# Gated attention's triangles on row tiles of the array, V on column tiles, and the softmax sums taken by ScalarE

## The chip, the core and the metric

One core of a Trainium2 chip runs the whole program, one launch for all 32 batch rows. The metric is the device time of that core in microseconds, from its first to its last instruction, with a little around it. Lower is better.

## What is computed

A decoder layer on x of shape 32 x 256 x 256 (row, token, feature), all in float32, with three residual blocks:

```
x = x + gated_attention(layernorm(x))      # 4 heads, 64 slots; q and k of 32, v of 64 per head
x = x + cross_attention(layernorm(x), ctx) # 16 heads of 16, ctx has 77 tokens a row, a mask of keys
x = x + moe(layernorm(x))                  # 8 experts of rank 64, the best 2 of 8 weighted
```

The gated attention runs two linear recurrences over the tokens, with slot weights exp(s - cumulative logsumexp(s)). The kernel writes each as a product with a causal triangle inside blocks of 128 tokens plus a state that is carried from the first block to the second. The first triangle is A = K Q^T per head (over 32 features), the second is P = E qn^T per head (over 64 slots, E = exp(s), qn the normalised softmax of the first result). In the cross attention, a softmax over 77 context tokens is taken for each of 16 heads, and its product with V is divided by the softmax's sum.

## The kernel before

**Stages.** A batch row goes through four stages, one per iteration: N (norm, projections, convolution of the gated attention), A (its attention and output), X (cross attention), F (mixture of experts). In iteration i the five instruction queues hold the N steps of row i, the A steps of row i-1, the X steps of row i-2 and the F steps of row i-3; there are 35 iterations. Each engine has its own function `body` with an order of these steps written out by hand, and runs them strictly in this order. Steps on different engines are tied by one semaphore per step. `upto(r, n)` is the count that a step with n increments a row has reached after row r. `g_mm`, `g_out`, `g_lo`, `g_store` project the context to K and V for all rows at once, during the first iterations.

**PSUM.** All eight banks of 128 x 512 float32 have fixed users: `E0` (all products of stage N, turns of E and v), `A0` and `A1` (stage A), `X0` (`x_turn`, `x_q`, the scores `x_s`, `x_proj`), `X1` (turned probabilities and turned output), `X2` (the product with V), `F0` and `F1` (stage F). So within X, everything that goes through `X0` follows one upon another: `x_turn` of a row can't start before `x_out` (VectorE) has read the `x_proj` of the row before.

**Products.** Projections split each operand in a high and a low half of type float32r and add three products (`mm_halves`). The others are float32 products, and each such product stands as two matmuls and two weight loads in the trace. `a_A` is one product of 128 x 512 per block c: the 32 features of each of 4 heads lie on the 128 partitions, and `q_bd` holds the four heads' q on a block diagonal of zeros, so that heads don't mix. `a_P` does the same with 64 slots and `qn_bd`, 256 columns at a time. VectorE multiplies both with a triangle (`a_maskA`, `a_maskP`).

**Cross attention.** A row has 8 units u = (c, q): a block c of 128 tokens and 4 heads. `x_s` makes the scores of a unit in `X0` (three matmuls of 308 columns), `x_soft` (VectorE) takes the maximum, `x_prob` (ScalarE) makes four exponentials of 128 x 77 into `prob`, where a head has 80 columns, and only then can `x_s` of the next unit overwrite `X0`. `x_pt` turns `prob` in 10 tiles of 128 columns a block, and `x_av` multiplies each turned tile, as the stationary operand, with the 34 or 51 columns of `Vbd` that its heads have: 16 features a head and a column of ones that gives the softmax's sum. `x_rs` and `x_o` (VectorE) divide, `x_ot` turns the output (TensorE) and copies it (ScalarE), `x_otl` makes the low half, `x_proj` projects.

**DMA.** One queue (SyncE) loads x and the mask, stores the output, and fills `Vbd` (12 small transfers a row) and the K tiles from a copy of K and V in HBM.

## Time and profile before

| | |
|---|---|
| median of 3 runs | 1520.54 us (1518.21 to 1521.38) |
| profiled execution | 1518.72 us |
| its span, first to last instruction | 1516.6 us |
| TensorE matmul busy | 96% |
| VectorE, ScalarE, GpSimdE busy | 80%, 63%, 55% |
| granted TensorE clock, mean | 0.989 of 2.4 GHz |

The profile is of one execution. A busy share says how much of the span had an instruction of the engine under way. Matmuls are pipelined and their ends are modelled, so a duration of a matmul is longer than its distance to the next; what a matmul costs is read from the distance of the starts. PE is TensorE, PEld its weight loads, DVE VectorE, ACT ScalarE, POOL GpSimdE, SP the DMA queue's engine.

### The profile page before, as it was taken

The numbers are of one execution on the slowest core, as the hardware profiler recorded it, in microseconds if no ns is written. First come the engines' busy times: TensorE is split into PE (matmuls) and PEld (weight loads), VectorE is DVE, ScalarE is ACT, GpSimd is POOL, SyncE is SP. The second block draws the span as 40 slices with busy tenths as digits, with TensorE's granted clock in tenths as the row PEclk, the third lists the DMA queues.
The fourth block names the chain that finished last, engine by engine and source line by source line (L and its number), as shares of the span: only waits on it lengthen the run. The fifth ranks groups of instructions, "written<-read, shape, count | busy, mean of one in ns | idle before, by whom it ended". The sixth has DMA issues, their size and how long they took to land.

```text
span 1516.6 us, 31405 instructions
## 1 busy us (share of the span) xinstructions
PE 1456.9 (96%) x10520; PEld 1291.4 (85%) x10520; DVE 1217.1 (80%) x3006; ACT 961.4 (63%) x2531; POOL 828.6 (55%) x937
## 2 busy tenths in 40 slices
PE   5798999999999999999999999999999999999975
PEld 3577989889889988988989888889988989989764
DVE  3668888888888888888888888888888888888642
ACT  3456666766666667666666766666667666666541
POOL 2355555656665565565556656655565565556420
PEclk9999999999999999999999999999999999999987
DMA  8230100011110001111100011110001111000000
GB/s 250 98 100 18 24 10 23 17 24 24 25 24 15 18 16 24 24 24 24 24 10 23 17 24 24 24 24 10 23 16 24 24 24 24 21 13 18 17 7 14
DMA packets 113102, 45.03 MB, mean 30 GB/s; under 512 B 86192, under 2 KB 109104, under 8 KB 112944
## 3 DMA queue, kind: packets, MB, share of 16 engines
q1 hardware_dynamic: 112944, 43.03, 11.3%
q8 instruction: 86, 1.41, 0.4%
q14 instruction: 72, 0.59, 0.1%
HBM read 26.74 MB, written 16.25 MB: 28 GB/s over the span
## 4 chain that ended last, share of the span: by engine, by line
PE 91%; DVE 3%; issue 2%; POOL 1%; ACT 1%; DMA 1%; SPq 0%; POOLq 0%; DVEq 0%; ACTq 0%
PE bank L444 76%; PE bank L450 7%; PE bank L685 5%; PE bank L770 2%; PE bank L532 1%; DVE a_conv L887 1%; PE bank L738 0%; DVE a_rC L909 0%; ACT x_prob L1331 0%; SPq L433 0%; DMA x_prob<-in_ctxT 0%; DVE x_nmax L1013 0%; DMA x<-in_x 0%; PE bank L541 0%; DVE x L1035 0%
## 5 line engine op out<-in xcount | busy, mean ns | idle before, releaser
L1331 ACT ACTIVATE x_prob<-bank,x_nmax 128x77 f32<-128x77 f32 x1024 | 248.5, 329 | 51.2 <-DVE x_nmax L1013 50.2
L1013 DVE TENSOR_REDUCE x_nmax<-bank 128x4 f32<-128x308 f32 x256 | 120.1, 469 | 109.8 <-PE bank L444 106.0
L1344 ACT ACTIVATE x_probT<-bank 128x256 f32<-128x256 f32 (+1 forms) x256 | 112.2, 438 | 98.3 <-PE bank L685 98.1
L1497 POOL TENSOR_TENSOR a_orinv<-a_ove,mhalf 128x8 f32<-128x8 f32 x32 | 65.1, 2035 | 199.1 <-DVE a_ove L952 199.1
L444 PE MATMUL bank<-x_Vbd,x_probT 128*128 128x34 f32 (+1 forms) x1280 | 162.5, 267 | 0.7 <-DVE x_o L1027 0.7
L887 DVE SCALAR_TENSOR_TENSOR a_conv<-a_raw,cw,a_conv 128x256 f32<-128x256 f32 x384 | 155.0, 478 | 7.5 <-POOL a_conv L1459 7.5
L444 PEld LDWEIGHTS bank<-x_Vbd,x_probT 128*128 128x128 f32 x1280 | 158.0, 192 | 1.1 <-DVE x_o L1027 1.1
L685 PE MATMUL bank<-ident,x_prob 128*128 128x128 f32 x640 | 114.6, 277 | 0.4 <-ACT x_prob L1331 0.3
L909 DVE RECIPROCAL a_rC<-bank 128x512 f32<-128x512 f32 x32 | 107.1, 3348 | 0.6 <-PE bank L444 0.6
L912 DVE TENSOR_TENSOR a_AT<-bank,tri 128x512 f32<-128x512 f32 x128 | 87.7, 685 | 23.9 <-PE bank L444 23.9
L444 PE MATMUL bank<-x_K_bd,x_Q_stack 128*128 128x308 f32 x256 | 94.5, 369 | 8.6 <-ACT x_prob L1331 5.2
L685 PEld LDWEIGHTS bank<-ident,x_prob 128*128 128x128 f32 x640 | 79.5, 145 | 21.9 <-ACT x_prob L1331 9.7
L1450 POOL TENSOR_SCALAR a_E<-a_E 128x512 f32<-128x512 f32 x32 | 62.1, 1940 | 54.9 <-ACT a_E L1230 54.9
L1459 POOL TENSOR_SCALAR a_conv<-a_raw,cw 128x256 f32<-128x256 f32 x128 | 59.1, 479 | 56.3 <-ACT a_raw L1224 56.3
L1535 POOL TENSOR_TENSOR f_s<-f_s,f_wt 128x512 f32<-128x512 f32 x64 | 66.7, 1043 | 39.0 <-DVE f_wt L1098 25.0
L1349 ACT ACTIVATE x_oT_hi<-bank 128x512 fp32r<-128x512 f32 x32 | 19.2, 598 | 107.2 <-PE bank L450 107.2
L1510 POOL TENSOR_TENSOR x_K_bd<-x_K_stack,groupmask 128x308 fp32r<-128x308 f32 x128 | 86.0, 704 | 0.0
L1434 POOL TENSOR_TENSOR x_rstd<-x_ve,mhalf 128x2 f32<-128x2 f32 x32 | 22.9, 715 | 114.6 <-DVE x_neg L842 114.6
L444 PE MATMUL bank<-x_negmask,ident_bf 128*128 128x308 bf16 x256 | 79.6, 311 | 0.0
L444 PE MATMUL bank<-x_KT_lo_bd,x_Q_stack 128*128 128x308 f32 x256 | 77.4, 302 | 0.0
L1513 POOL TENSOR_TENSOR x_KT_lo_bd<-x_KT_lo,headmask 128x616 fp32r<-128x616 f32 x64 | 76.8, 1221 | 0.0
L444 PE MATMUL bank<-fwo_hi,f_sT_hi 128*128 128x256 f32 x256 | 75.2, 294 | 1.5 <-ACT f_sT_hi L1378 1.5
(271 smaller groups left out, 5264.0 us busy)
## 6 DMA issues: line engine op xcount, KB each, us to landing
x<-in_x SPq DMA_DIRECT2D x32, 256.0 KB, 2.6
out<-x SPq DMA_DIRECT2D x32, 256.0 KB, 2.2
x_K_stack<-k_hi SPq DMA_DIRECT2D x64, 77.0 KB, 2.6
k_hi<-f_sT_hi SPq DMA_DIRECT2D x5, 512.0 KB, 2.8
k_lo<-f_sT_lo SPq DMA_DIRECT2D x5, 512.0 KB, 3.8
v_tok<-x_probT SPq DMA_DIRECT2D x10, 256.0 KB, 3.4
x_KT_lo<-k_lo SPq DMA_DIRECT2D x32, 77.0 KB, 2.3
x_Vbd<-v_tok SPq DMA_DIRECT2D x128, 9.6 KB
```

The costliest lines, as they stand in the source:

```text
L444: return pe.matmul(out, lhsT, rhs, start=start, stop=stop, skip_group_check=True)
L450: ins = pe.transpose(dst[:, k * T + c * P:k * T + (c + 1) * P], src[:, c, k * P:(k + 1) * P], ident[:])
L685: ins = pe.transpose(X1[:, i * P:(i + 1) * P], prob[:, t * P:(t + 1) * P], ident[:])
L887: stt(conv[:, j, :], raw[:, j, i:i + T], cw[:, j, i:i + 1], conv[:, j, :], ALU.mult, ALU.add).then_inc(on.a_conv, 1)
L909: dve.reciprocal(flat(rC[r % 2]), E0[:, :]).then_inc(on.a_rC, 1)
L912: return tt(dst, src.rearrange("p (h t) -> p h t", h=H), tri.rearrange("p (o t) -> p o t", o=1).broadcast_to([P, H, P]), ALU.mult)
L1013: dve.tensor_reduce(nmax[:, u % 2, :], X0[:, 0:UH * S2].rearrange("p (h s) -> p h s", h=UH), AX.X, ALU.min).then_inc(on.x_max, 1)
L1331: ins = act.activation(prob[:, col:col + S2], X0[:, i * S2:(i + 1) * S2], ACT.Exp, scale=-1.0, bias=nmax[:, u % 2, i:i + 1])
L1344: act.activation(probT[:, g[0]:g[-1] + 1, :].rearrange("p h t -> p (h t)"), X1[:, 0:len(g) * P], ACT.Copy).then_inc(on.x_pT, 1)
L1510: pool.tensor_tensor(K_bd[:, q], K_stack[r % 2][:, q:q + 1, :].broadcast_to([P, UH, S2]), spread(groupmask[:], S2), ALU.mult)
L1513: ins = pool.tensor_tensor(KT_lo_bd[:, f], KT_lo[r % 2][:, f:f + 1, :].broadcast_to([P, HB, S2]), spread(headmask[:], S2), ALU.mult)
L1535: pool.tensor_tensor(fs[:, c, :].rearrange("p (e q) -> p e q", e=NE), fs[:, c, :].rearrange("p (e q) -> p e q", e=NE), spread(wt[:, c, :], ...
```

## The change

- `a_A` and `a_P` no longer use a block diagonal over all partitions. Each product takes 64 partitions (`rows`), the upper and the lower half in turn, and writes the upper's result to one bank and the lower's to the other: 4 products of 256 columns for `a_A`, 8 of 128 columns for `a_P`. `q_bd` shrinks to two heads a half, `qn_bd` and `qn_last` become one plain copy `qnT`. Both blocks of a row are now one step.
- `x_av` swaps its operands: `Vbd` (64 columns, four heads, zeros elsewhere) is stationary and `probT`, which now holds both blocks' tokens, moves with 256 columns. The output has 64 partitions (the column tile i) and is already turned. There are 12 products a row in 2 steps, in place of 20 in 8.
- The column of ones goes. `x_prob` gives each exponential an accumulator output, `xsum`. VectorE takes its reciprocal (`x_rs`), GpSimdE spreads it over the 16 features of a head (`x_rse`), TensorE turns that (`x_rt`, four turns in place of those of `x_ot`), ScalarE copies it, and VectorE multiplies the product with V by it (`x_on`); the high half is then copied from SBUF (`x_ot`).
- `a_conv`, `a_rc`, `f_yy` and `x_kbd` are cut in pieces that other steps can stand between.
- Every engine has a new order. On TensorE, `x_proj` moves from the end of an iteration to the beginning of the next, `a_ktok` the other way, and the turns `x_pt` start later. On SyncE, `Vbd` is filled last in an iteration, for a row of stage N.

```diff
-VW = 3 * (HD + 1)
+VS, VW = 6, 4 * HD
...
-        q_bd = [sb(f"a_q_bd_{i}", [P, H, T]) for i in range(2)]
+        q_bd = [sb(f"a_q_bd_{i}", [P, 2, T]) for i in range(2)]
...
-        AT = sb("a_AT", [P, TC, H, P])
+        AT = sb("a_AT", [P, 2, TC * 2, P])
...
-        qn_bd = sb("a_qn_bd", [P, 2, 2, T])
-        qn_last = sb("a_qn_last", [P, 2, P])
+        qnT = sb("a_qnT", [P, 2, T])
...
-        g_ctx = [sb(f"g_ctx_{i}", [P, GW]) for i in range(3)]
-        Vbd = [sb(f"x_Vbd_{i}", [P, NT, VW]) for i in range(2)]
+        Vbd = [sb(f"x_Vbd_{i}", [P, 2, VS, VW]) for i in range(2)]
...
-        probT = sb("x_probT", [P, NT, P])
+        probT = sb("x_probT", [P, NT, T])
+        xsum = sb("x_sum", [P, TC, NH])
         xrs = sb("x_rs", [P, TC, NH])
-        xo = sb("x_o", [P, TC, D])
+        rse = sb("x_rse", [P, TC, D])
+        rsT = sb("x_rsT", [P, KC, T])
+        xo = sb("x_o", [P, KC, T])
...
-            (Vbd[0][:], a["vones"]), (Vbd[1][:], a["vones"]),
...
-                N(g_store, 0); N(g_store, 1); N(x_load); N(g_store, 2); N(g_store, 3); L(a_load); A(x_vbd)
-                F(f_store); N(x_kin)
+                N(g_store, 0); N(x_load); N(g_store, 1); N(g_store, 2); N(g_store, 3); L(a_load); F(f_store)
+                N(x_kin); N(x_vbd)
...
-            def a_A(r, c):
...
+            def a_A(r):
+                pe.wait_ge(on.a_qbd, upto(r))
+                if r > 0:
+                    pe.wait_ge(on.a_oT, upto(r - 1))
+                    pe.wait_ge(on.a_oTl, upto(r - 1))
+                pe.wait_ge(on.a_ktok, upto(r))
+                for c in range(TC):
+                    for i in range(2):
+                        rows = slice(i * P // 2, (i + 1) * P // 2)
+                        ins = mm((A0 if i == 0 else A1)[:, c * D:(c + 1) * D], qkr[r % 2][rows, 1, c * P:(c + 1) * P],
+                                 q_bd[r % 2][rows, :, c * P:(c + 1) * P])
+                        if c == TC - 1:
+                            ins.then_inc(on.a_A_ps, 1)
...
-            def a_P(r, c):
...
+            def a_P(r):
+                pe.wait_ge(on.a_qnT, upto(r))
+                for c in range(TC):
+                    for f in range(2):
+                        for i in range(2):
+                            rows = slice(i * P // 2, (i + 1) * P // 2)
+                            ins = mm((A1 if i == 0 else A0)[:, c * D + f * P:c * D + (f + 1) * P],
+                                     ET[r % 2][rows, f, c * P:(c + 1) * P], qnT[rows, f, c * P:(c + 1) * P])
+                            if c == TC - 1 and f == 1:
+                                ins.then_inc(on.a_P_ps, 1)
...
-            def x_av(r, u):
-                c, q = divmod(u, QU)
-                if u == 0:
+            def x_av(r, g):
+                if g == 0:
                     if r > 0:
-                        pe.wait_ge(on.x_o, upto(r - 1, TC))
+                        pe.wait_ge(on.x_on, upto(r - 1))
                     else:
                         pe.wait_ge(on.g_v, 2 * NG)
                     pe.wait_ge(vbd_in[r % 2], loaded(r, len(V_PIECES)))
-                elif q == 0:
-                    pe.wait_ge(on.x_o, upto(r, TC, c))
-                pe.wait_ge(on.x_pT, upto(r, NU, u + 1))
-                for t in GROUPS[q]:
-                    h, w = first_head(t) * (HD + 1), tile_heads(t) * (HD + 1)
-                    ins = mm(X2[:, h:h + w], probT[:, t, :], Vbd[r % 2][:, t, 0:w], start=(t == 0),
-                             stop=(t == NT - 1))
+                pe.wait_ge(on.x_pT, upto(r, NU, QU + 2 * (g + 1)))
+                for j in range(VS // 2):
+                    for i in range(2):
+                        t = g * NT // 2 + 2 * i + j
+                        ins = mm(X2[i * VW:(i + 1) * VW, g * T:(g + 1) * T], Vbd[r % 2][:, g, i * VS // 2 + j, :],
+                                 probT[:, t, :], start=(j == 0), stop=(j == VS // 2 - 1))
                 ins.then_inc(on.x_av_ps, 1)
-            def x_ot(r):
-                pe.wait_ge(on.x_o, upto(r, TC))
-                turn(X1, xo).then_inc(on.x_oT_ps, 1)
+            def x_rt(r):
+                pe.wait_ge(on.x_rse, upto(r, TC))
+                pe.wait_ge(on.x_pT, upto(r, NU))
+                for f in range(KC):
+                    for c in range(TC):
+                        ins = pe.transpose(X1[:, f * T + c * P:f * T + (c + 1) * P],
+                                           rse[:, c, f * P:(f + 1) * P], ident[:])
+                ins.then_inc(on.x_rT_ps, 1)
...
-                A(a_vtok); N(g_mm, 0); N(g_mm, 1); A(a_ktok); A(a_A, 0); X(x_turn); A(a_A, 1); A(a_state)
-                N(g_mm, 2); N(a_turn); X(x_q); F(f_turn); A(a_ok); N(a_qk); X(x_s, 0); F(f_gate); F(f_u0)
-                N(g_mm, 3); X(x_pt, 0); X(x_s, 1); F(f_lg); N(a_v); A(a_qt); X(x_s, 2); F(f_v0); N(a_s)
-                X(x_s, 3); A(a_P, 0); A(a_P, 1); X(x_pt, 1); X(x_av, 0); X(x_s, 4); X(x_pt, 2); A(a_o)
-                X(x_av, 1); X(x_pt, 3); F(f_st, 0); X(x_s, 5); N(g_mm, 4); N(a_g); F(f_u1); X(x_pt, 4)
-                X(x_av, 2); X(x_s, 6); F(f_v1); X(x_pt, 5); X(x_av, 3); N(g_mm, 5); X(x_s, 7); N(g_mm, 6)
-                N(a_c); X(x_pt, 6); A(a_ot); N(g_mm, 7); X(x_av, 4); F(f_st, 1); X(x_pt, 7); X(x_av, 5)
-                X(x_av, 6); X(x_av, 7); N(a_et); A(a_wo); X(x_ot); F(f_yy); X(x_proj)
+                F(x_proj); A(a_vtok); A(a_A); N(g_mm, 0); X(x_turn); A(a_state); N(g_mm, 1); X(x_q); N(a_turn)
+                F(f_turn); A(a_ok); X(x_s, 0); F(f_gate); N(a_qk); F(f_u0); N(g_mm, 2); X(x_s, 1); F(f_lg)
+                N(a_v); N(g_mm, 3); A(a_qt); X(x_s, 2); F(f_v0); N(a_s); X(x_s, 3); X(x_pt, 0); A(a_P)
+                X(x_pt, 1); X(x_s, 4); X(x_pt, 2); A(a_o); X(x_s, 5); X(x_pt, 3); N(a_g); X(x_pt, 4)
+                F(f_st, 0); X(x_s, 6); F(f_u1); X(x_pt, 5); N(g_mm, 4); F(f_v1); X(x_s, 7); X(x_pt, 6)
+                X(x_av, 0); N(g_mm, 5); N(g_mm, 6); N(a_c); X(x_pt, 7); A(a_ot); F(f_st, 1); X(x_av, 1)
+                N(g_mm, 7); X(x_rt); A(a_wo); F(f_yy, 0); F(f_yy, 1); N(a_et); N(a_ktok)
...
-            def a_rc(r):
+            def a_rc(r, c):
                 dve.wait_ge(on.a_C_ps, upto(r))
                 if r > 1:
                     dve.wait_ge(on.a_qn, upto(r - 2))
-                dve.reciprocal(flat(rC[r % 2]), E0[:, :]).then_inc(on.a_rC, 1)
+                dve.reciprocal(rC[r % 2][:, c, :], E0[:, c * D:(c + 1) * D]).then_inc(on.a_rC, 1)
...
-                dve.wait_ge(on.x_av_ps, upto(r, NU, (c + 1) * QU))
...
+                dve.wait_ge(on.x_prob, upto(r, NU, (c + 1) * QU))
+                if r > 0:
+                    dve.wait_ge(on.x_rse, upto(r - 1, TC))
+                dve.reciprocal(xrs[:, c, :], xsum[:, c, :]).then_inc(on.x_rs, 1)
+            def x_on(r):
+                dve.wait_ge(on.x_av_ps, upto(r, 2))
+                dve.wait_ge(on.x_rT, upto(r))
+                if r > 0:
+                    dve.wait_ge(on.x_oT, upto(r - 1))
+                    dve.wait_ge(on.x_oTl, upto(r - 1))
+                tt(flat(xo), X2[:, :], flat(rsT), ALU.mult).then_inc(on.x_on, 1)
...
+                N(a_stats); N(a_mv); F(x_out); N(a_ve); F(f_stats); A(a_maskA, 0); F(f_mv); F(f_ve); X(x_xntl)
...
+                X(x_soft, 3); F(f_s, 0); A(a_maskP, 0); A(a_maskP, 1); X(x_soft, 4); N(a_conv, 1, 1)
+                N(a_conv, 2, 0); N(a_conv, 2, 1); X(x_rs, 0); F(f_wt); X(x_soft, 5); A(a_oss); N(a_conv, 3, 0)
+                N(a_conv, 3, 1); A(a_ove); X(x_soft, 6); F(f_stl, 0); N(a_gate); N(g_lo, 2); A(a_o1)
+                F(f_su, 1); X(x_soft, 7); F(f_s, 1); N(a_silu_qk); N(g_lo, 3); X(x_rs, 1); N(a_rot)
+                N(a_rc, 0); A(a_otl); F(f_stl, 1); N(a_rc, 1); X(x_on); A(a_out); N(a_silu_v); X(x_otl)
+                A(x_stats); A(x_mv); A(x_ve); F(f_out)
...
-                src = A0[:, :].rearrange("p (f t) -> p f t", f=2)
-                for hh in range(2):
-                    s = slice(hh * M, (hh + 1) * M)
-                    act.activation(qn_bd[s, :, hh, :], src[s], ACT.Copy).then_inc(on.a_qnT, 1)
-                act.activation(qn_last[:], src[:, :, P:2 * P], ACT.Copy).then_inc(on.a_qnT, 1)
+                act.activation(flat(qnT), A0[:, :], ACT.Copy).then_inc(on.a_qnT, 1)
...
-                                         bias=nmax[:, u % 2, i:i + 1])
+                                         bias=nmax[:, u % 2, i:i + 1], accum_out=xsum[:, c, q * UH + i:q * UH + i + 1])
...
+            def x_rt(r):
+                act.wait_ge(on.x_rT_ps, upto(r))
+                if r > 0:
+                    act.wait_ge(on.x_on, upto(r - 1))
+                act.activation(flat(rsT), X1[:, :], ACT.Copy).then_inc(on.x_rT, 1)
             def x_ot(r):
-                act.wait_ge(on.x_oT_ps, upto(r))
-                act.activation(flat(xoT[0]), X1[:, :], ACT.Copy).then_inc(on.x_oT, 1)
+                act.wait_ge(on.x_on, upto(r))
+                if r > 0:
+                    act.wait_ge(on.x_proj_ps, upto(r - 1))
+                act.activation(flat(xoT[0]), flat(xo), ACT.Copy).then_inc(on.x_oT, 1)
...
+                A(a_vtok); X(x_xnt); N(a_xn); F(f_xn); X(x_q); N(a_xnt); F(f_xnt); X(x_prob, 0); N(g_out, 0)
...
+                X(x_prob, 7); X(x_pt, 7); N(g_out, 5); N(g_out, 6); A(a_ot); F(f_st, 1); X(x_rt)
+                N(a_convt, 1); N(g_out, 7); X(x_ot); N(a_qbd); N(a_et); N(a_ktok); A(x_xn)
...
+            def x_rse(r, c):
+                pool.wait_ge(on.x_rs, upto(r, TC, c + 1))
+                if r > 0:
+                    pool.wait_ge(on.x_rT_ps, upto(r - 1))
+                pool.tensor_scalar(rse[:, c, :].rearrange("p (h e) -> p h e", h=NH), spread(xrs[:, c, :], HD),
+                                   1.0, 1.0, ALU.mult, ALU.mult).then_inc(on.x_rse, 1)
...
+                X(x_kbd, 0); X(x_kbd, 1); X(x_rstd); X(x_kbd, 2); N(a_rstd); X(x_neg); F(f_rstd); X(x_kbd, 3)
+                X(x_kbd, 4); X(x_kbd, 5); X(x_x1b); A(a_oks); A(a_qn); N(a_tap0); N(a_clip); F(f_sw, 0)
+                X(x_rse, 0); A(a_orinv); N(a_elo); A(a_o2); F(f_sw, 1); X(x_rse, 1); N(a_cos); N(a_sin)
+                N(a_kr)
...
-            pool.memset(qn_bd[:], 0.0).then_inc(z_ready, 1)
+            for i in range(2):
+                pool.memset(Vbd[i][:], 0.0).then_inc(v_zero, 1)

```

## Rows read from the trace of the kernel before

**Rows 1.** The page: busy time of each engine, then the chain that ended last.

```profile
PE 1456.9 (96%) x10520; PEld 1291.4 (85%) x10520; DVE 1217.1 (80%) x3006; ACT 961.4 (63%) x2531; POOL 828.6 (55%) x937
...
PE 91%; DVE 3%; issue 2%; POOL 1%; ACT 1%; DMA 1%; SPq 0%; POOLq 0%; DVEq 0%; ACTq 0%
```

**Rows 2.** Windows, one period: length, then each engine's busy time and instructions, clock.

```profile
753.60:797.40 43.80, 43.80 (x327) 39.36 (x326) 37.39 (x93) 29.33 (x79) 25.69 (x30) 1.00 0.09 21
```

**Rows 3.** The page's costliest groups: the product with V.

```profile
L444 PE MATMUL bank<-x_Vbd,x_probT 128*128 128x34 f32 (+1 forms) x1280 | 162.5, 267 | 0.7 <-DVE x_o L1027 0.7
```

**Rows 4.** Windows, TensorE: the six stretches of x_av in one period, first and sum.

```profile
768.62:768.98 0.36, 0.36 (x6) 1.00 0.00 0
...
sum 4.17, PE 4.17; mean PE 0.69
```

**Rows 5.** Windows, TensorE: a_P, then the two blocks of a_A, same period.

```profile
766.56:768.29 1.73, 1.73 (x11) 1.00 0.00 0
792.28:793.14 0.86, 0.86 (x5) 1.00 0.15 13
793.58:794.53 0.95, 0.95 (x4) 1.00 0.08 8
```

**Rows 6.** Timeline, TensorE, around f_lg: start, duration, line, operands (stationary on the right).

```profile
760.52 0.31 PE L444 MATMUL bank<-x_negmask,ident_bf 128*128 128x308 bf16 x1
760.76 0.29 PE L738 MATMUL bank<-ident,f_lgT 16*128 16x16 f32 x2
760.98 0.39 PE L444 MATMUL bank<-a_xnT_hi,wv_hi 128*128 128x256 f32 x1
761.20 0.28 PE L444 MATMUL bank<-a_xnT_lo,wv_hi 128*128 128x256 f32 x1
```

**Rows 7.** Timeline, TensorE: x_s(0), x_s(1), x_s(7), x_proj, x_turn, next x_s(0).

```profile
757.62 0.30 PE L444 MATMUL bank<-x_K_bd,x_Q_stack 128*128 128x308 f32 x1
...
760.15 0.39 PE L444 MATMUL bank<-x_K_bd,x_Q_stack 128*128 128x308 f32 x1
...
780.00 0.39 PE L444 MATMUL bank<-x_K_bd,x_Q_stack 128*128 128x308 f32 x1
...
790.31 0.28 PE L444 MATMUL bank<-xwp_hi,x_oT_hi 128*128 128x256 f32 x1
...
793.14 0.60 PE L450 MATMUL bank<-ident,x_xn 128*128 128x128 f32 x4
...
801.49 0.30 PE L444 MATMUL bank<-x_K_bd,x_Q_stack 128*128 128x308 f32 x1
```

**Rows 8.** Timeline, ScalarE: the last x_prob and x_pt of the row.

```profile
781.92 0.97 ACT L1331 ACTIVATE x_prob<-bank,x_nmax 128x77 f32<-128x77 f32 x4
...
783.78 0.49 ACT L1344 ACTIVATE x_probT<-bank 128x384 f32<-128x384 f32 x1
```

**Rows 9.** Groups by shape, ScalarE, one period: busy time, mean ns, idle before.

```profile
L1331 ACT ACTIVATE x_prob<-bank,x_nmax 128x77 f32<-128x77 f32 x32 | 7.8, 328 | 1.3 <-DVE x_nmax L1013 1.2
...
L1282 ACT ACTIVATE a_qn_bd<-bank 64x512 f32<-64x512 f32 x2 | 1.2, 585 | 0.0
...
L1364 ACT ACTIVATE f_egap<-f_gap 128x2 f32<-128x2 f32 x1 | 0.2, 220 | 0.0
```

**Rows 10.** Groups by shape, VectorE, one period.

```profile
L912 DVE TENSOR_TENSOR a_AT<-bank,tri 128x512 f32<-128x512 f32 x5 | 3.4, 684 | 0.6 <-PE bank L444 0.6
L909 DVE RECIPROCAL a_rC<-bank 128x512 f32<-128x512 f32 x1 | 3.3, 3347 | 0.0
...
L1027 DVE TENSOR_TENSOR x_o<-bank,x_rs 128x256 f32<-128x256 f32 x2 | 0.8, 416 | 0.0
```

**Rows 11.** Groups by shape, GpSimdE, one period.

```profile
L1459 POOL TENSOR_SCALAR a_conv<-a_raw,cw 128x256 f32<-128x256 f32 x4 | 1.8, 479 | 1.4 <-ACT a_raw L1224 1.4
```

**Rows 12.** Timeline, GpSimdE, start of the program.

```profile
3.48 0.95 POOL L1563 MEMSET a_qn_bd<- 128x1024 f32 x1
14.55 0.71 POOL L1434 TENSOR_TENSOR a_rstd<-a_ve,mhalf 128x2 f32<-128x2 f32 x1 [10.12 <-DVE a_neg L842]
```

176 lines of the change are left out of this document (62 added, 114 removed).

## The prediction

> **What bounds the kernel now.** I began with the page's busy times and its chain [rows 1]: TensorE is busy 96% of the span and holds 91% of the chain that ended last. Then I looked at single periods. One row takes 43.8 us once all four stages run, and TensorE has work under way in all of it, at full clock, while VectorE has 37.4 us, ScalarE 29.3 and GpSimdE 25.7 [rows 2]. So the time is 32 rows times what TensorE must do for one, plus the first and last iterations, in which stages are missing. A busy share alone can't say that, since ends of matmuls are modelled; the timeline's starts can, and they follow on each other without holes of over a few tenths. Next in line are VectorE at 37.4 us and a loop that no busy share shows: all of stage X passes through the bank `X0`. From one `x_s(0)` to the next the loop goes 757.62, 760.15, ... 780.00 (`x_s(7)`), 790.31 (`x_proj`), 793.14 (`x_turn`), 801.49 [rows 7]. It fills the period, but partly because its steps queue behind others.
>
> **What a float32 pass costs.** Each float32 product stands as two passes. `a_P` is 4 products of 256 columns, 8 passes, 1.73 us [rows 5], or 0.216 us a pass; block 0 of `a_A` is two passes of 512 columns in 0.86 us, 0.43 each. So a pass takes 2 cycles of 2.4 GHz a column. `x_av` has 1280 / 32 = 40 passes a row [rows 3] of only 34 or 51 columns, in 4.17 us [rows 4], 0.104 us a pass. That is over twice the 28 to 43 ns of its columns, and about what loading 128 stationary columns would take at the same 2 cycles: the product with V is bound by its weight loads.
>
> **The products after.** The number of columns that move, with no overlap of tiles: `a_A` 4 products of 256, 8 passes of 0.213, 1.71 us as before; `a_P` 8 products of 128, 16 passes of 0.107, 1.71 as before; `x_av` 12 products of 256, 24 passes, 5.12 us, 0.95 more. All gain must come from two tiles working at once. No instruction of the trace of before works beside another on a part of the array, so I bound it: nothing, or half of each (0.86, 0.86, 2.56 us: 0.86 + 0.86 + 1.61 = 3.3 us saved). Between these I take what an in-order queue gives if a pass waits only for its own tile. The queue holds both passes of the upper tile, then both of the lower. The second upper pass runs beside the first lower, the second lower beside the next upper, and n products take n + 1 passes instead of 2n. `a_A`: 5 x 0.213 = 1.07, saves 0.65. `a_P`: 9 x 0.107 = 0.96, saves 0.77. `x_av`: two steps of 7 x 0.213 = 2.98, saves 1.19. Sum 2.6 us a row. A weaker point is `a_P`: 16 loads of 128 columns at the 0.104 us of [rows 4] are 1.7 us if loads go one after another, and its gain is then nothing; for `x_av`, with 64 columns a load, and `a_A`, with 8 loads, that bound is not reached.
>
> **Changing the tiles' shape.** Four steps a row now enter and leave another shape of tile (`a_A`, `a_P`, `x_av` twice): 8 changes. The nearest row is `f_lg`, which uses 16 partitions: it starts 0.24 us after a matmul of 308 columns (0.13 us at full clock), and the 256-column matmul behind it is followed after 0.22 us, where its columns need 0.11 [rows 6]. That is 0.1 us on either side. Bounds: 0, since such a gap could belong to any change of operand, and 0.17 a change, the 0.31 us duration of [rows 6] less those columns, if everything must drain. I take 0.1 each, 0.8 us a row. The Trainium skill (TensorEngine Tiling (Array Packing), Key Properties) says that changing the mode, not just the tile, drains the engine; by it all 8 changes cost, and a full drain each would be 1.4 us instead of 0.8. The trace's 0.1 on both sides of `f_lg` agrees in sign.
>
> **Other parts on TensorE.** `x_rt` has the four turns of `x_ot`. `x_proj`, `a_ktok` and the turns `x_pt` are moved but are the same work. Holes: `a_state` now waits for a mask (VectorE) that stands behind `x_out` and the statistics, and `x_proj` opens an iteration and waits for `x_otl`, with only `a_wo`, `f_yy`, `a_et` and `a_ktok` ahead of it. I take 0.4 us a row more of holes (bounds 0 and 1.5, the latter if both are in full late by one 512-column VectorE step of 0.68 [rows 10]). Behind a waiting `x_proj` stand `a_vtok` and `a_A`, and for them wait ScalarE's `a_vtok` and the masks.
>
> **ScalarE.** 32 exponentials a row (328 ns each, 0.97 us for four [rows 8, 9]) now also deliver a sum. No row shows an accumulator. Bounds: 0, and 0.22 us each if it were a small instruction of its own, such as `f_egap` on 2 columns [rows 9]. I take 0.1: it is smaller than a whole instruction, as neighbours overlap (four of 0.328 take 0.97). That is 3.2 us; `x_rt` adds one copy of about 0.59, and `a_qnt` loses at least one of its two such copies [rows 9]. ScalarE goes to some 32.5 us (36.4 at the bound), hidden under TensorE. What it costs there is latency in the loop, below.
>
> **VectorE and GpSimdE.** `x_on` (0.68) replaces two `x_o` (0.83) [rows 10]. The reciprocal of 3.35 us is cut in two and can't gain more than it lets others pass. VectorE stays at 37.4, hidden with 4 us to spare. GpSimdE gets two `x_rse` of about 0.48 [rows 11], 26.7 us, hidden; each queues behind `f_sw` or ahead of `a_orinv`. At the start it clears two `Vbd` of 3072 columns, three times 0.95 us each, 5.7 in place of 0.95, from 3.5 to 9.2; its next work began at 14.55 [rows 12], so that costs nothing. On SyncE the fill of `Vbd` moves to the end of the iteration behind the store and the K tiles, and is for a row that needs it two iterations later: a hold-up there has a period to spare. `a_load` keeps its place ahead of the store; the two `vones` loads go. I count nothing.
>
> **The sum.** 2.6 - 0.8 - 0.4 = 1.4 us a row less: a period of 42.4 us. 32 x 1.4 = 45 us from the profiled execution's 1518.7 gives 1474; the median of runs is 1.8 us above that execution, so the forecast is 1476 us.
>
> **Rival 1: tiles overlap fully.** Savings of 3.3 - 0.8 = 2.5 us a row on TensorE give a period of 41.3, but the X loop comes near (below), so I take 41.4 to 42: about 2.2 x 32 = 70 us, 1450; with no loss at the changes and no holes, 3.3 x 32 = 106, 1415. For it: nothing in before speaks of order inside the array. Against: two passes of one product must both use one tile. The Trainium skill (TensorE: Matmul & The Clock Gate, Part 3: Packing small matmuls) says that matmuls on different tiles start about 4 ns apart, so a pair takes the time of one; by it the sum would be this rival's. No run here shows it.
>
> **Rival 2: the X loop becomes the bound.** Shortest distance of two `x_s` before: 2.53 us [rows 7], 7 of them 17.7. From `x_s(7)` to `x_proj` after: 2.9 to the end of the exponentials (780.00 to 782.89, [rows 7, 8]), 0.33 turns, 0.49 copy, 1.5 for the second `x_av`, 0.44 turns, then copy, `x_on`, copy, `x_otl` of about 0.6 to 0.7 each, and some 0.7 for eight hand-overs: 9.0. `x_proj` to `x_turn` 2.8 and on to `x_s(0)` 8.35 as before [rows 7]. Sum 37.9, plus 32 times the accumulator's price d. With d = 0.1 it is 41.1, under 42.4; it takes over from d = 0.14, and at 0.22 is 44.9, less what the 8.35 can give. The period is then 43.5 to 44: 1510 to 1530. For it: 8.35 holds queueing but no step was taken out of it. Against: a small output read is hardly a whole instruction.
>
> **Rival 3, slower: tiles don't overlap.** If float32 passes on two tiles go one after another, `x_av` costs 0.95 more and the changes of shape 0.8: 1.75 us a row, 56 us, 1576. For it: two cycles a column already make float32 special, and all three gains hang on this. Against: halves of the array with separate operands and banks share nothing that the trace shows. It decides as soon as overlap saves under 1.8 us a row of the 3.3.
>
> **Rival 4: loads in line.** `a_P` gains nothing (0.77 less): 0.6 us a row, 19 us, 1500.
>
> **Chances.** Forecast 0.40 (own range 1458 to 1492), rival 1 0.17, rival 2 0.15 (a third of it faster), rival 4 0.12, rival 3 0.16. Low end: rival 1 between its two values, 1432. High end: rival 2's high value and some, 1540, which leaves rival 3 (0.16) and a little below out. A difference of 0.2% is what can be told from none here. Faster 0.40 + 0.17 + 0.12 + 0.05 = 0.74, less 0.01 for holes larger than taken, 0.73; same 0.07; slower 0.20.
>
> **What would show it.** `a_A` near 1.1 us a row from first to next start, `a_P` near 1.0, `x_av` near 1.5 a step; 1.7, 1.7 and 2.6 would be rival 3, 0.9, 0.9 and 1.3 rival 1. A gap of 0.1 at each change. Four exponentials in 1.4 us, not 0.97. TensorE waits in steady state for `x_prob` or `x_otl` mean rival 2. The prediction is wrong if the overlap isn't there or if the accumulator costs over 0.14 us.

## The result, and the profile after

The changed kernel takes 1503.64 us (median of 8 runs, 1498.5 to 1511.65) against 1520.59 for the kernel before (8 runs). The ratio is 0.9894 with a 95% interval of 0.9865 to 0.9922: 1.1% faster, where 2.9% was forecast. The profiled execution took 1503.3 us, its span is 1501.5. The eight runs follow the mean granted clock: the three at 0.986 to 0.989 took 1498.5 to 1499.5 us, the two at 0.982 took 1503.3 and 1504.0, the three at 0.975 to 0.978 took 1507.7 to 1511.7; the kernel before is at 0.989. First the page (busy times, chain that ended last), to be held against [rows 1]:

```profile
PE 1410.3 (94%) x10392; PEld 1200.0 (80%) x10392; DVE 1206.6 (80%) x3006; ACT 1036.0 (69%) x3523; POOL 860.8 (57%) x1002
...
PE 69%; DVE 18%; issue 4%; ACT 4%; SPq 2%; POOL 1%; DMA 1%; POOLq 0%; ACTq 0%
```

TensorE lost 22 points of the chain and VectorE gained 15. Windows over four periods, from the start of one `a_A` to the next (as [rows 2]):

```profile
652.07:695.33 43.26, 42.31 (x322) 36.51 (x321) 37.15 (x94) 31.83 (x110) 26.89 (x32) 1.00 0.10 22
695.33:738.30 42.97, 42.11 (x322) 36.35 (x321) 36.40 (x92) 31.58 (x110) 26.68 (x32) 1.00 0.09 22
738.30:782.18 43.88, 42.17 (x323) 36.35 (x322) 37.65 (x95) 31.72 (x110) 26.82 (x32) 1.00 0.09 21
782.18:825.37 43.19, 42.26 (x323) 36.48 (x322) 37.13 (x94) 31.81 (x110) 26.88 (x32) 1.00 0.09 21
```

Mean period 43.3 us; three periods of before, cut the same way, have 43.8 with TensorE busy in all of it. Now 1.1 us of each has no matmul under way, at full clock. Matmul ends are modelled, so the starts tell more: I gave each group of matmuls its own pitch and took the rest up to the next start as a gap. Before: 42.2 us of work and 1.6 of gaps a row; after: 39.3 to 39.6 and 3.7 to 4.0. TensorE's work fell by 2.6 to 2.9 us a row and its gaps grew by 2.1 to 2.4. This split is an estimate, since a pitch (the distance of two starts within a group) had to be chosen for each group.

Starts alone give a firmer account. Over twenty rows, from the seventh start of `a_A` to the twenty-seventh, the period is 43.80 us before and 43.12 after: 0.68 us a row, which would be 22 us over 32 rows. Whole runs show 17. The difference lies in the first and last rows. From its second start to its third `a_A` takes 46.6 us where before it took 42.4, and inside this time the granted clock is at its lower level (1.2 GHz) for 3.4 us, which can explain 1.7 us at most (an estimate: half of them). First the whole time, then that stretch; the clock stands before the last two numbers:

```profile
88.46:135.10 46.64, 41.03 (x281) 32.69 (x281) 31.26 (x66) 29.61 (x104) 24.04 (x29) 0.96 0.18 52
122.50:125.90 3.40, 3.40 (x16) 1.81 (x15) 2.77 (x5) 1.65 (x10) 2.60 (x4) 0.51 0.00 0
```

From the last start of `a_A` to the end it is 116.2 us, 43 of them at the lower clock, where before it was 111.0, 29 of them at the lower clock.

The timeline of TensorE shows that the products did what they were meant to do (to be held against [rows 4, 5]):

```profile
738.30 1.14 PE L437 MATMUL bank<-a_q_bd,a_qkr 64*128 64x256 f32 x8
...
757.67 0.38 PE L683 MATMUL bank<-ident,x_prob 128*128 128x128 f32 x2
757.99 1.16 PE L437 MATMUL bank<-a_qnT,a_ET 64*128 64x128 f32 x16
759.08 0.33 PE L683 MATMUL bank<-ident,x_prob 128*128 128x128 f32 x1
...
770.03 1.51 PE L437 MATMUL bank<-x_probT,x_Vbd 128*64 128x256 f32 x12
771.48 0.39 PE L437 MATMUL bank<-a_Er_hi,tri 128*128 128x256 f32 x1
```

`a_P` takes 1.09 us to the next start instead of 1.73, a step of `x_av` 1.45, two of them 2.90 instead of 4.17; `a_A` takes 1.14 at most (1.06 where nothing follows late, below) instead of 0.86 + 0.95. Each of these steps also starts late. A pass of 128 columns like the two at 757.67 is followed by the next after 0.11 us, but where a step of tiles follows, after 0.20 (757.78 to 757.98 here, and 0.20 in each of 24 rows). So entering costs 0.09 us ahead of each of the four steps, 0.37 a row, and this is in the gaps and not in the times just given.

The waits of TensorE show part of what came instead (us in all, times, longest; before had 5.2 us for `x_prob`, and 0.8 us once for `a_AT`):

```profile
PE bank L437 <- DVE a_AT L909: 21.7, 31, 1.4
PE bank L437 <- ACT x_prob L1327: 8.7, 16, 1.6
```

`a_state` waits 0.7 us a row for the first mask. The chain, followed back through one period, says why (start, us, what):

```profile
741.62 2.69 PE bank L437 x18
...
757.87 0.49 DVE x_nmax L1010
...
758.61 1.12 ACT x_prob L1327 x7
...
775.10 0.13 PE bank L706
775.23 0.60 DVE f_sT_lo L1112
775.83 0.65 DVE a_rC L906
776.47 0.93 issue
777.40 0.64 DVE x_o L1025
778.03 0.60 DVE x L964
...
781.05 0.59 DVE x L1116
781.64 0.67 DVE a_stats L827 x2
```

From 775.2 us the chain leaves TensorE and stays on VectorE for 9.5 us. VectorE's own timeline has no idle time from `x_on` to `a_maskA`; each step starts as soon as the one ahead lets it:

```profile
777.40 0.64 DVE L1025 TENSOR_TENSOR x_o<-bank,x_rsT 128x512 f32<-128x512 f32 x1
777.95 0.69 DVE L964 TENSOR_TENSOR x<-bank,x 128x512 f32<-128x512 f32 x1
...
779.14 0.69 DVE L854 TENSOR_TENSOR x_oT_lo<-x_o,x_oT_hi 128x512 fp32r<-128x512 f32 x1
...
780.96 0.68 DVE L1116 TENSOR_TENSOR x<-bank,x 128x512 f32<-128x512 f32 x1
781.56 0.74 DVE L827 BATCH_NORM_STATS2 a_stats<-x 128x6 f32<-128x256 f32 x2
782.50 0.66 DVE L1032 TENSOR_TENSOR x<-bank,x 128x512 f32<-128x512 f32 x1
783.21 0.75 DVE L827 BATCH_NORM_STATS2 f_stats<-x 128x6 f32<-128x256 f32 x2
783.87 0.68 DVE L909 TENSOR_TENSOR a_AT<-bank,tri 128x512 f32<-128x512 f32 x1
```

The accumulator outputs are instructions of their own. The page's groups:

```profile
L1327 ACT ACTIVATE x_prob<-bank,x_nmax 128x77 f32<-128x77 f32 x1024 | 318.7, 327 | 143.1 <-DVE x_nmax L1010 140.7
L1327 ACT ACTIVATION_READ_ACCUMULATOR x_prob<-bank,x_nmax 128x1 f32 x1024 | 210.5, 206 | 0.0
```

### The profile page after: what moved, and what is told of

Same layout as the page of the kernel before. It is cut to its first block, busy times and chain, and to the rows that moved or that the text cites. A ratio compares the mean times of both kernels' runs of the same rounds, so it can differ in the third digit from the quotient of the medians.

```text
span 1501.5 us, 32796 instructions
## 1 busy us (share of the span) xinstructions
PE 1410.3 (94%) x10392; PEld 1200.0 (80%) x10392; DVE 1206.6 (80%) x3006; ACT 1036.0 (69%) x3523; POOL 860.8 (57%) x1002
## 4 chain that ended last, share of the span: by engine, by line
PE 69%; DVE 18%; issue 4%; ACT 4%; SPq 2%; POOL 1%; DMA 1%; POOLq 0%; ACTq 0%
PE bank L437 59%; PE bank L443 4%; PE bank L683 4%; ACT x_prob L1327 3%; PE bank L771 2%; DVE a_rC L906 1%; DVE x L1032 1%; DVE f_stats L827 1%; DVE a_stats L827 1%; DVE x_o L1025 1%; DVE x_stats L827 1%; DVE a_AT L909 1%; DVE x_nmax L1010 1%; DVE x L964 1%; DVE x L1116 1%
## 5 line engine op out<-in xcount | busy, mean ns | idle before, releaser
L1327 ACT ACTIVATE x_prob<-bank,x_nmax 128x77 f32<-128x77 f32 x1024 | 318.7, 327 | 143.1 <-DVE x_nmax L1010 140.7
L1327 ACT ACTIVATION_READ_ACCUMULATOR x_prob<-bank,x_nmax 128x1 f32 x1024 | 210.5, 206 | 0.0
L1543 POOL TENSOR_TENSOR f_s<-f_s,f_wt 128x512 f32<-128x512 f32 x64 | 77.7, 1214 | 177.2 <-DVE f_wt L1095 138.1
L884 DVE SCALAR_TENSOR_TENSOR a_conv<-a_raw,cw,a_conv 128x256 f32<-128x256 f32 x384 | 165.1, 491 | 6.8 <-POOL a_conv L1461 6.8
L906 DVE RECIPROCAL a_rC<-bank 128x256 f32<-128x256 f32 x64 | 111.7, 1746 | 1.3 <-PE bank L437 1.3
L437 PE MATMUL bank<-x_probT,x_Vbd 128*64 128x256 f32 x768 | 98.3, 392 | 0.3
L1491 POOL TENSOR_TENSOR a_okn<-a_okn,a_okmax 128x512 f32<-128x512 f32 x32 | 33.4, 1044 | 98.7 <-DVE a_okmax L927 98.7
L999 DVE SCALAR_TENSOR_TENSOR x_Q_stack<-bank,x_Q_stack 64x512 fp32r<-64x512 f32 x64 | 44.1, 688 | 54.5 <-ACT x_Q_stack L1312 54.0
L1499 POOL TENSOR_TENSOR a_orinv<-a_ove,mhalf 128x8 f32<-128x8 f32 x32 | 53.4, 1670 | 45.2 <-DVE a_ove L949 45.2
L437 PEld LDWEIGHTS bank<-x_probT,x_Vbd 128*64 128x64 f32 x768 | 49.9, 138 | 30.1 <-issue 11.1
```

The costliest lines, as they stand in the source:

```text
L437: return pe.matmul(out, lhsT, rhs, start=start, stop=stop, skip_group_check=True)
L884: stt(conv[:, j, :], raw[:, j, i:i + T], cw[:, j, i:i + 1], conv[:, j, :], ALU.mult, ALU.add).then_inc(on.a_conv, 1)
L906: dve.reciprocal(rC[r % 2][:, c, :], E0[:, c * D:(c + 1) * D]).then_inc(on.a_rC, 1)
L1327: ins = act.activation(prob[:, col:col + S2], X0[:, i * S2:(i + 1) * S2], ACT.Exp, scale=-1.0, bias=nmax[:, u % 2, i:i + 1], accum_out=xsu ...
L1543: pool.tensor_tensor(fs[:, c, :].rearrange("p (e q) -> p e q", e=NE), fs[:, c, :].rearrange("p (e q) -> p e q", e=NE), spread(wt[:, c, :], ...
```

## Experiments

Each ratio is to the kernel before on the same chip (medians 1519.1 to 1522.0 us). "The changed kernel" is 1503.6 us, in its own eight runs, with an interval of 0.9865 to 0.9922; an experiment whose interval meets this one (e6, e7, e11, e15, e16) can't be told from it by its whole time alone.

**e1_serial.** All three products with the loops turned, so that one tile's passes are all issued before the other's.

```diff
 a_A:            -for c, for i      +for i, for c
 a_P:            -for c, for f, i   +for i, for c, f
 x_av:           -for j, for i      +for i, for j
```

> The changed kernel with the loops over the two tiles turned inside out, so that all products of the upper tile stand ahead of all of the lower; the sum is the same. Theory (a pass waits only for its own tile, in-order queue): only one pair of passes per step can overlap. a_A goes from 5 to 7 passes of 0.213 us (+0.43), a_P from 9 to 15 of 0.107 (+0.64), the two x_av steps from 7 to 11 passes of 0.213 each (+1.70): 2.8 us of TensorE work a row more. Some of it falls into waits that TensorE has anyway at the start of an iteration (0.4 of a_A), so the period goes from 43.1 to about 45.4 us and the time from 1503 to about 1577 us; an x_av step takes 2.35 us instead of 1.45. Rival (the tiles' queues are independent, order within a step doesn't matter): no change, 1503 us.

Measured: 1541.03 us, ratio 1.0135 [1.0116, 1.0155]. `a_P` went to 1.64 us and a step of `x_av` to 1.93, but `a_A` stayed at 1.1. Two narrow windows of the timeline, the first 0.2 us of `a_P` in the changed kernel, then in this one:

```profile
757.99 0.38 PE L437 MATMUL bank<-a_qnT,a_ET 64*128 64x128 f32 x2
```

```profile
780.56 0.37 PE L437 MATMUL bank<-a_qnT,a_ET 64*128 64x128 f32 x1
```

In the changed kernel the passes start in pairs, 7 ns apart (757.985 and 757.992, then 758.199 and 758.205), not one pass behind the other. In e1_serial the second tile's first pass started 6 ns behind the fifth of the first tile's eight in `a_P` (781.111, 781.117), 6 ns behind the third of six in `x_av` (748.461, 748.467), and 13 ns behind the first of four in `a_A` (761.090, 761.103): each time with three passes of the other tile issued before it and still to start. So overlap depends on order, as said, but here a pass overtook three. Both my theory's time (1577) and the rival's (order doesn't matter, 1503) are wrong. Issuing the tiles in turn is worth 37 us; what the overlap is worth as a whole isn't measured, since a part of it is still there in this run.

**e2_noacc.** No accumulators; the sums are set to 1 once, so the output isn't normalised.

```diff
-    bias=nmax[:, u % 2, i:i + 1], accum_out=xsum[:, c, q * UH + i:q * UH + i + 1])
+    bias=nmax[:, u % 2, i:i + 1])
```

> The changed kernel without the accumulator output of the exponentials; the sums are a constant 1 written once, so the output is not normalised. It prices the accumulator. Theory (the accumulator costs ScalarE 0.09 us an exponential, 2.8 us a row, but is mostly hidden; what holds the row is VectorE's queue around the start of an iteration): at most 0.3 us a row faster, 1493 to 1503 us. Rival (the loop through bank X0 binds, and the accumulator lengthens it by 0.09 x 32 = 2.8 us): 1.5 us a row or more faster, 1455 us or less.

Measured: 1490.74 us, 0.9813 [0.9798, 0.9829]. The accumulators cost 13 us, 0.4 us a row, just under the range of the theory and far from the rival. It is not hidden, though ScalarE has 11 us a row to spare. The traces show where it acts. In the changed kernel VectorE waits 0.21 us a row for the last `x_prob` before it starts `x_rs`, and from there to the first mask its queue has 0.1 us of idle time in 11.7 (medians of 24 rows). Without accumulators `x_rs` starts 0.6 us sooner behind `x_s(7)`, and `x_on`, further down the queue, 0.44 us sooner against `x_rt` (1.94 us behind it for 2.38).

**e3_order.** `x_out` and the mask ahead on VectorE.

```diff
-N(a_stats); N(a_mv); F(x_out); N(a_ve); F(f_stats); A(a_maskA, 0); F(f_mv); F(f_ve); X(x_xntl)
+F(x_out); N(a_stats); A(a_maskA, 0); N(a_mv); N(a_ve); F(f_stats); F(f_mv); F(f_ve); X(x_xntl)
```

> The changed kernel with only VectorE's first steps in another order: x_out, a_stats, a_maskA(0), a_mv, a_ve, f_stats in place of a_stats, a_mv, x_out, a_ve, f_stats, a_maskA(0). Theory (the overlap's gain turned into TensorE waits for x_out, 0.70 us, and for a_maskA, 0.82 us, a row): x_out starts 0.65 us earlier and a_maskA 0.5 us, together about 1.1 us a row less, a period of 42.0, 1468 us. Rival (the row is held by the loop of scores and exponentials, and the next wait takes over): within 0.2 us a row, 1497 to 1503 us.

Measured: 1525.84 us, 1.0040 [1.0025, 1.0056]: 22 us slower than the changed kernel. TensorE's wait for the mask fell to 8.3 us and another took its place:

```profile
PE bank L437 <- DVE x_xnT_lo L854: 34.7, 31, 1.5
```

**e4_rowtiles.** The kernel before with the row tiles of `a_A` and `a_P` alone, in the old order (`q_bd`, `AT`, `qnT` as in the change).

> The kernel before with the row tiles alone: a_A and a_P as in the change, in the place of their first halves, and one copy qnT; everything else, the order too, as before. Theory (TensorE's queue bound the kernel before, with under 1 us of holes in a period of 43.7): a_A 0.65 and a_P 0.64 us less work, of which 1.1 us a row reach the end, 1485 us. Rival (VectorE's stretch around the start of an iteration was as long as TensorE's already, so less work there turns into a wait): under 0.3 us a row, 1510 us or more.

Measured: 1520.72 us, 1.0009 [0.9999, 1.0018]: no gain, as the rival's number said. Over twenty rows `a_A` and `a_P` take 1.4 us a row less from start to next start, and the period is 43.9 us. TensorE waits where it never did before:

```profile
PE bank L443 <- ACT a_ktok L1270: 16.6, 32, 0.6
...
PE bank L443 <- DVE a_AT L917: 11.5, 33, 1.4
```

The first of these waits is made by this kernel's own change: block 0 of `a_A` needed no `a_ktok` before, and the step for both blocks does. It stands right behind the turn that `a_ktok` copies, and 0.68 us a row are lost there, 0.5 at `a_state`. So this run doesn't test the theory cleanly. Nor does its page show the rival's mechanism, since VectorE holds little of the chain that ended last:

```profile
PE 53%; POOL 19%; issue 19%; DVE 5%; ACT 3%; SPq 0%; DMA 0%; POOLq 0%; ACTq 0%; DVEq 0%
```

**e5_order2.** The same start of VectorE's order, with what e3_order had missed.

```diff
+N(a_stats); F(x_out); N(a_mv); N(a_ve); A(a_maskA, 0); F(f_stats); X(x_xntl); F(f_mv); F(f_ve)
```

> The changed kernel with another order of VectorE's first instructions: a_stats, x_out, a_mv, a_ve, a_maskA of half 0, f_stats, x_xntl, f_mv, f_ve. The earlier reordering lost 1.29 us a row at TensorE's wait for x_xntl, because x_xntl stood behind a_mv, a_ve, f_stats, f_mv and f_ve, all held up by the first triangle; here x_xntl stands right behind f_stats and nothing small is behind the triangle. Theory (TensorE's holes of 0.93 us ahead of a_state's neighbour and 0.32 us ahead of x_turn are local waits that an earlier instruction closes): 0.6 to 0.9 us a row less, 1475 to 1484 us. Rival (VectorE's queue from 769.7 to 784.5 us has no hole and sets the length of the row as a whole, so that the order within it only moves the wait): 1498 to 1508 us.

Measured: 1514.59 us, 0.9969 [0.9955, 0.9982], 11 us slower than the changed kernel. `f_stats` is now late, and TensorE waits for `f_xn`: 20.7 us over 32 times.

**e6_short_rc, e7_pe_proj, e8_pe_s.** What one engine's time is worth at one place: VectorE 1.31 us less, TensorE 0.47 us more behind `a_wo`, the same ahead of `a_s`.

```diff
 e6 (a_rc, c == 1)
-dve.reciprocal(rC[r % 2][:, c, :], E0[:, c * D:(c + 1) * D])
+ts(rC[r % 2][:, c, :], E0[:, c * D:(c + 1) * D], 1.0, None, ALU.mult)
 e7 (f_yy, c == 0)
+for _ in range(4): mm(F0[:, 0:D], fsT[0][:, 0, 0, :], fwo[0][:, 0, :])
 e8 (a_s)
+for _ in range(4): mm(E0[:, 0:D], xnT["a"][0][:, 0, 0:P], ws[0][:, 0, :])
```

> The changed kernel with the reciprocal of the second half of C replaced by a copy of the same 256 columns, so that this half is multiplied by C where it should be divided: 1.66 us of VectorE's queue become about 0.35 us, in the middle of the stretch from 769.7 to 784.5 us that has no hole. Theory (this stretch of VectorE sets the length of the row, with TensorE waiting 2.1 us a row more than in the kernel before): 1.3 us a row less, about 1461 us. Rival (VectorE is late only by chance of single waits, TensorE's work is the bound): 1495 to 1503 us.

> The changed kernel with four products more on TensorE per row, 0.47 us, ahead of f_yy of half 0 (at 776.9 us of the profile, beside VectorE's stretch without a hole). Theory that VectorE's stretch sets the length of the row there: no change, 1500 to 1506 us. Rival that TensorE's queue does: 32 times 0.47 = 15 us more, 1518 us.

> The changed kernel with the same four products, 0.47 us a row, ahead of a_s, in the middle of the row, where TensorE shows no idle time for 14 us. Theory that the chain of a row leaves TensorE only in the last third: 15 us more, 1518 us. Rival (another engine's chain runs beside the middle of the row too): less than 5 us more.

Measured: e6 1496.25 us, 0.9844 [0.9821, 0.9867]; e7 1509.64, 0.9935 [0.9921, 0.9950]; e8 1514.76, 0.9966 [0.9950, 0.9981]. So 15 us of TensorE work cost 11 in the middle of a row (nearer the theory of e8) and 6 at its end (between the theory and the rival of e7), and 42 us off VectorE gave 7. The intervals of e6 and e7 touch that of the changed kernel, but the steady rows say the same: periods of 42.8 us (e6), 43.2 (e7) and 43.5 (e8) against 43.1. The time of e6 lies in its rival's range, far from the theory's 1461. The trace of e6 shows where the rest of the 1.31 us a row went, VectorE then GpSimdE:

```profile
729.35 0.69 DVE L1028 TENSOR_TENSOR x_o<-bank,x_rsT 128x512 f32<-128x512 f32 x1 [0.24 <-issue]
730.08 0.69 DVE L967 TENSOR_TENSOR x<-bank,x 128x512 f32<-128x512 f32 x1
731.28 1.19 DVE L854 TENSOR_TENSOR x_oT_lo<-x_o,x_oT_hi 128x512 fp32r<-128x512 f32 x1
```

```profile
730.03 1.89 POOL L1515 TENSOR_TENSOR x_K_bd<-x_K_stack,groupmask 128x308 fp32r<-128x308 f32 x2
```

Counted from the start of `x_rt` on TensorE, `x_on` (the first line) comes 1.0 us earlier than in the changed kernel and then waits for ScalarE's copy of `x_rt`. `a_out` (the second line) comes 0.8 us earlier and starts 0.2 us behind the last columns of `a_wo`, which it needs, so what stands ahead of it in VectorE's queue can give no more. Then `x_otl` met GpSimdE's `x_K_bd`, in 29 of 32 rows, and both took 0.5 us longer (0.69 and 1.37 when apart). What stands behind `x_otl` comes 0.3 us earlier, and the period is 0.3 us shorter.

**e9_early_proj.** `x_proj` between the halves of `f_yy`, with `x_out` and `f_stats` following early on VectorE, the second `a_rc` behind `x_ve`, and F ahead of N on the other engines.

```diff
-A(a_wo); F(f_yy, 0); F(f_yy, 1); N(a_et); N(a_ktok)
+A(a_wo); F(f_yy, 0); X(x_proj); F(f_yy, 1); N(a_et); N(a_ktok)
```

> The changed kernel with another order of steps around the end of an iteration, and nothing else: x_proj stands between the two halves of f_yy on TensorE, its result x_out and f_stats follow it before f_out and a_stats on VectorE, the second a_rc goes behind x_ve, and POOL, ScalarE and TensorE take f_rstd, f_xn, f_turn ahead of a_rstd, a_xn, a_turn. Theory (after the savings TensorE has too little other work, 2.05 us, between the end of x_proj and a_state to cover the chain x_proj, x_out, f_stats, first triangle, and the same for f_xn and f_turn; taking 1.31 us off VectorE's queue alone gave 0.28 us a row because this chain starts with TensorE): with x_proj 1.4 us earlier the holes of 0.92 and 0.27 us close, 0.6 to 1.0 us a row less, 1471 to 1484 us. Rival (VectorE has no time left from 769.7 to 784.5 us whatever the order, so another wait takes the place as in the two orders tried before): 1498 to 1520 us.

Measured: 1573.8 us, 1.0357 [1.0330, 1.0384], worse than the rival allowed. The new waits:

```profile
PE bank L437 <- DVE x_oT_lo L854: 23.6, 32, 1.7
PE bank L525 <- ACT a_ET L1257: 22.4, 31, 0.7
```

`a_et` waits for the later `a_rc`, ScalarE's `a_ET` for it, and `a_vtok` for that.

**e10_av_serial.** `x_av` alone with its loops turned.

> The changed kernel with the loops of x_av alone turned inside out, so that one column tile's six passes are issued before the other's. In the run with all three loops turned, a step of x_av took 1.93 us instead of 1.45 and a_P 1.64 instead of 1.09, a_A the same 1.1. Theory (x_av lies on the chain of the row through x_rse and x_on): 2 times 0.48 us a row, up to 31 us more, 1525 to 1535 us. Rival (x_av lies beside VectorE's stretch without a hole and is covered by it): less than 10 us more.

Measured: 1523.82 us, 1.0028 [1.0015, 1.0041]: 20 us of the 31 show, between the two. `x_av` is largely on the chain.

**e11_half_yy and e12_half_yy_rc.** `f_yy` sums over two of its four blocks (the output lacks the rest); e12 has e6's copy as well.

```diff
-for i in range(RC)]).then_inc(on.f_y_ps, 1)
+for i in range(RC // 2)]).then_inc(on.f_y_ps, 1)
```

> The changed kernel without the second half of the gated feed-forward's last product (f_yy sums over two of its four column blocks), so that 12 of TensorE's products, 1.4 us a row, are gone from the stretch beside VectorE's queue without a hole; the output lacks that half of the sum. Theory (x_proj behind them waits for x_otl, which VectorE ends at 779.8 us against 780.13 for x_proj's start, so TensorE's savings of this size come back as a wait): 0.3 us a row, 1490 to 1500 us. Rival (TensorE's work is the bound, the holes are accidents of single steps): 1.4 us a row, 1459 us.

> The same, and VectorE's second reciprocal replaced by a copy as before (which alone gave 7 us): TensorE is 1.4 us a row shorter and VectorE 1.3 us, in the same stretch. Theory (two chains side by side, each of which hides the other's savings): more than the sum of the two alone, 1.2 us a row or more, 1455 to 1470 us. Rival (the two savings are independent): the sum of the two alone, 1483 to 1493 us if the first of them gave 3 to 13 us.

Measured: e11 1501.61 us, 0.9895 [0.9867, 0.9922]: 45 us of TensorE work are gone and the time is that of the changed kernel. TensorE waits for `x_otl` instead (the second wait is the one of the changed kernel):

```profile
PE bank L437 <- DVE x_oT_lo L854: 28.6, 31, 1.5
PE bank L437 <- DVE a_AT L909: 21.2, 30, 1.4
```

e12: 1494.48 us, 0.9822 [0.9790, 0.9854], no more than e6 alone. My theory that the two hide each other's savings falls: the mask comes as late as in e6, though TensorE has 1.4 us less to do beside VectorE's steps. Here `x_otl` met `x_K_bd` in 9 of 32 rows only and yet e12 isn't faster than e6; why not stays open.

**e13_late_out and e14_late_out_noacc.** `f_out` of a row goes behind `a_maskA` of half 1 in the next iteration; e14 adds e2's edit.

```diff
-A(x_stats); A(x_mv); A(x_ve); F(f_out)
+A(x_stats); A(x_mv); A(x_ve)
...
 A(a_state); A(a_maskA, 1)
+if rf: f_out(rf - 1)
```

> The changed kernel with f_out of a row moved out of VectorE's stretch at the end of an iteration, behind the second first-triangle mask of the next one, where VectorE waits 1.7 us a row (54.0 us over 32 rows) for x_Q_stack anyway; nothing else moves. Theory (a second chain sets the row: TensorE from a_state to a_wo, then VectorE's eleven operations from a_out to the first triangle, 7.1 to 7.2 us, while TensorE has 6.2 us or less of work behind a_wo): VectorE's part is 0.6 us shorter, up to the 0.57 us that the end of a_A allows: 12 to 19 us less, 1485 to 1492 us. Rival (every earlier move only made another wait, and this one delays f_out and the row's store and transposition f_turn behind it): 1500 to 1515 us.

> The same with the exponentials' accumulators left out and the sums set to 1 once (the output isn't normalised). Without the move this gave 13 us. Theory (the exponentials lie in the other part of the same chain, from a_state to a_wo, so the two add up): 24 to 32 us less than the changed kernel, 1472 to 1480 us. Rival (the two hide each other): within 5 us of the better one alone.

Measured: e13 1498.78 us, 0.9843 [0.9829, 0.9856], 5 us better than the changed kernel where 12 to 19 were worked out, just outside the rival's range. e14 1487.91 us, 0.9784 [0.9769, 0.9799], 16 us better, 3 us under e2_noacc and so within 5 us of the better one alone, as the rival said; the 24 to 32 of the theory are missed. In e13's VectorE timeline the next row's load is what is late (the longest of 29 such waits, 10.7 us in all):

```profile
741.04 0.75 DVE L827 BATCH_NORM_STATS2 a_stats<-x 128x6 f32<-128x256 f32 x2 [1.50 <-DMA x<-in_x]
```

**e15_three_x and e16_three_x_alone.** Three buffers `x0` and three semaphores `ld_x` instead of two, with and without the late `f_out`.

```diff
-x0 = [sb(f"x0_{i}", [P, TC, D]) for i in range(2)]
+x0 = [sb(f"x0_{i}", [P, TC, D]) for i in range(3)]
-if r > 1: sp.wait_ge(on.a_x1, upto(r - 2))
+if r > 2: sp.wait_ge(on.a_x1, upto(r - 3))
```

> The kernel with the late f_out, and a third buffer for the rows of x, so that a row's load starts an iteration earlier and no longer when a_out frees its buffer. With the late f_out alone VectorE had its work behind a_out done at 739.4 us and then waited 1.50 us for the load that was issued at 737.1 (a_stats at 741.04), and the chain that ended last has 5% of the span at this load. Theory (with VectorE's part shorter the load, a_out to a_stats, is the next on the same chain): up to the 0.57 us a row of the earlier move that didn't show, 10 to 17 us less than 1499, 1482 to 1489 us. Rival (the load is only late in a few rows, where another transfer is beside it): 1495 to 1500 us.

> The changed kernel with the third buffer for the rows of x and f_out where it is. Theory (with f_out ahead of a_stats the load has landed in all but one to three of 32 rows): 0 to 3 us less, 1500 to 1504 us. Rival (the load is on the chain there too): 1488 to 1496 us.

Measured: e15 1497.08 us, 0.9855 [0.9838, 0.9871]; e16 1501.83, 0.9879 [0.9863, 0.9896]. The theory of e16 holds: with `f_out` in its old place the load is late in 3 of 32 rows of the changed kernel. The rival of e15 has the time right and not the reason, since in e13 the load is late in 29 rows, by little. The third buffer takes these waits away and the period falls by 0.1 us. The chain of e15 is another (page; then followed back through the end of a row):

```profile
PE 83%; DVE 6%; ACT 6%; issue 3%; POOL 1%; SPq 1%; DMA 1%; POOLq 0%; ACTq 0%; DVEq 0%
```

```profile
739.36 1.06 PE bank L437 x8
...
740.50 0.64 PE bank L443 x4
...
741.17 0.61 ACT x_xnT_hi L1308
...
741.80 0.70 DVE x_xnT_lo L854
...
742.63 1.67 PE bank L437 x12
```

VectorE's stretch is gone from it, and what is left between `a_A` (1.06 us) and `x_q` is, beside `a_state`, the latency of `x_turn`, a copy and `x_xntl`. e15 computes the whole layer and is the fastest such kernel here, 1.5% under the kernel before; e13 can't be told from it.

**One row in two parts.** The traces allow one more comparison. Each row is divided at two starts on TensorE, that of `x_rt` and that of the next `a_state`. These are medians of 24 rows, in us:

| run | what it changes | `x_rt` to `a_state` | `a_state` to next `x_rt` | period |
|---|---|---|---|---|
| changed kernel | | 9.67 | 33.4 | 43.08 |
| e7_pe_proj | TensorE +0.47 in the first part | 9.68 | 33.5 | 43.21 |
| e11_half_yy | TensorE -1.37 in the first part | 9.67 | 33.4 | 43.07 |
| e8_pe_s | TensorE +0.47 in the second part | 9.68 | 33.8 | 43.49 |
| e6_short_rc | VectorE -1.31 ahead of `x_on` | 9.37 | 33.4 | 42.77 |
| e12_half_yy_rc | both, e11 and e6 | 9.43 | 33.4 | 42.84 |
| e2_noacc | ScalarE -0.09 an exponential | 9.23 | 33.5 | 42.77 |
| e15_three_x | one step and one load out of VectorE's stretch | 9.23 | 33.6 | 42.87 |

In the first part TensorE's own work doesn't matter, neither more nor less of it, and a VectorE queue that is shorter or starts sooner shortens it. In the second part TensorE's work shows nearly in full (0.4 of 0.47). In e15 the second part is 0.2 us longer, since `x_q` then waits longer for `x_xntl` (0.42 us from the matmul ahead of it, 0.18 in the changed kernel): this is the next chain, and it takes back half of the gain.

## Why the prediction was wrong

- **What bounds the kernel.** Right for before, wrong as a ground for what follows. "The time is 32 rows times what TensorE must do" holds only as long as no other chain comes within the savings. In e4_rowtiles 1.4 us a row of TensorE's work less gained nothing in the old order, though half of that went into a wait that its own change of the steps made.
- **The products after.** Near in size, wrong in mechanism. Passes pair off fully, which was rival 1's mechanism; "a pass waits only for its own tile" in a strictly ordered queue was wrong. Full pairs save 3.3 us a row. Of this, 0.3 is lost because the second pass of a step comes late (0.21 us behind the first in `a_P`, where later ones are 0.11 apart; 0.32 for 0.22 in `a_A`; 0.27 for 0.22 in each `x_av`). That leaves 3.0, where n + 1 passes gave 2.6. The Trainium skill (TensorE: Matmul & The Clock Gate, Part 3: Packing small matmuls) has starts about 4 ns apart, the trace 7; its sentence that matmuls start in strict order is not what e1_serial shows.
- **Changing the tiles' shape.** Right: 0.09 us to enter and 0.09 to leave each of the four steps, 0.75 a row of the forecast 0.8. From its start to the next start `a_A` saves 0.75, `a_P` 0.64 and `x_av` 1.27, 2.7 in all; the exits are in these times, the entries (0.37) stand ahead of them. Net it is 2.3 us a row, where the forecast had 1.8.
- **Loads in line (rival 4), no overlap (rival 3).** Neither: `a_P` is at 1.09, and its weight loads come in pairs 7 ns apart like its passes. That the measured 1503.6 lies beside rival 4's 1500 is chance.
- **The step that failed: holes, "0.4 us a row more (bounds 0 and 1.5)".** Over the twenty rows they were 1.6, over the bound (2.3 saved, 0.68 left). By starts, 0.86 of it stands ahead of `a_state`, 0.14 ahead of `x_turn`, 0.31 ahead of `x_s(4)` and 0.29 ahead of `f_gate`. I had named the right wait, `a_state` behind the mask behind `x_out` and the statistics, and priced it as one late step. It is the end of a chain: `x_s(7)` on TensorE, the last `x_prob` on ScalarE, then VectorE's queue from `x_rs` to the first triangle, 11.7 us with 0.1 of idle time. From the end of `a_wo` at 776.9 us to the end of the mask at 784.5 VectorE's queue has 7.6 us without a hole (the rest of `a_rc` and `x_on`, 1.0 us, then 6.6 from `a_out` on), while TensorE has 6.8 of its own by its pitches (`f_yy` 2.7, `x_proj` 1.5, `a_A` 1.1, the turns 1.4). I had said VectorE was hidden "with 4 us to spare"; that is true over the row and false in this stretch. The table of the two parts shows it: 1.4 us a row of TensorE's work less beside this stretch gave nothing, and each run that moved VectorE's steps forward (e2, e6, e12, e15) made the period 0.2 to 0.3 us shorter. More than that of the 1.0 us ahead of `a_state` and `x_turn` no run got back.
- **The accumulator.** Its price was right: four exponentials stand 0.305 us apart instead of 0.213, 0.09 each (forecast 0.1). "Hidden under TensorE" was wrong: e2_noacc gives 0.4 us a row, and its first part in the table is 0.44 shorter. It was rival 2's ingredient, but not its loop: it delays the last `x_prob` and with it the start of VectorE's stretch at `x_rs`, and the period of 43.1 isn't reached by the sum 41.1 of the `X0` loop.
- **The sum.** In a full row 3.0 from the overlap, less 0.75 for the changes, less 1.6 of holes: 0.7 us, where the working had 2.6, 0.8 and 0.4. The overlap was 0.4 too small, the holes 1.2. The working also took this for 32 equal rows; the first and last rows gave about 5 us back, with the clock at its lower level for longer.

Open: why `x_s(4)` and `f_gate` come later than before. Three of my theories about which order closes the gaps fell (e3, e5, e9), and e13 and e15 gave a third or less of what they promised; for e15 the table shows the next chain, for e3, e5 and e9 only the new waits are known. What column tiles for V give in the old order wasn't tried, nor what the new order gives without the tiles, so how much of the holes comes from the order that was written with the change isn't measured. Why the clock is lower in the first and last rows isn't either.

## What to carry to other kernels

Before costing savings on the engine that is always busy, find the second longest chain: at the stretch where the saved work lay, add up the other engines' steps from the last result that engine gives to the first that it needs back. Where that sum is within the savings, only the difference is won. Shortening or repeating one step measures this sooner than reordering does, above all when the row is divided at two events and each part is compared by itself. A queue that is idle for 15% of the row can still be the bound where its steps stand in one stretch.

## What the runs showed of the hardware

- Float32 passes on two tiles of the array, issued in turn, start 7 ns apart and run together. Issued one tile after the other (e1_serial), the second tile's first pass overtook exactly three waiting passes of the first, in all three products; so four per tile in a row (`a_A`) still pair off, 13 ns apart.
- A step on tiles of 64 rows or 64 columns starts 0.09 us late behind a product on the whole array, and the next product on the whole array 0.09 us late behind it.
- An exponential with an accumulator output is two instructions, the second of 206 ns, and takes 0.09 us more of ScalarE (0.305 from start to start in place of 0.213).
- VectorE's `x_otl` (two SBUF operands) and GpSimdE's `x_K_bd` each took 0.5 us longer when they met (0.69 to 1.19 us, 1.37 to 1.89). The Trainium skill (SBUF — State Buffer, section "SBUF: two separate sides") says that a VectorE operation with two SBUF inputs and a GpSimdE one that reads SBUF exclude each other, and that the one that starts first has the port for the whole instruction. The trace agrees that they hinder each other; but the `x_K_bd` that had started 0.6 us earlier took 0.5 us longer too (0.70 to 1.23).
